# A four-layer graph network on one core: one row per node, product tables and chains down the partitions in place of transposed scans over an edge list

## The reference, cut to what matters

```python
x = ln(x + segment_sum((x @ W0)[src] * rsqrt(deg_out[src]) * rsqrt(deg_in[dst]), dst) + b0)   # layer 0
def conv(x, Wm, We, Wr, b):
    agg = segment_max(x[src] @ Wm + edge_attr @ We, dst)          # 0 for nodes without edges
    return leaky_relu(agg + x @ Wr + b)
x = ln(x + conv(conv(x, W1m, W1e, W1r, b1), W2m, W2e, W2r, b2))   # layer 1, halves a and b
m = relu(x[src]) + 1e-7
a = segment_softmax(m, dst)                                       # per feature
x = ln(x + (x + segment_sum(a * m, dst)) @ Wg + bg)               # layer 2
h = x @ Wa                                                        # layer 3: attention with self loops
x = ln(x + tanh(sum over edges and self of softmax(leaky_relu(a_src[src] + a_dst[dst])) * h[src] + ba))
```

## Time and profile before

| | |
|---|---|
| runs | 5404.59, 5427.97, 5431.95 us (median 5427.97) |
| profiled execution, span from first to last instruction | 5313.3 us |
| median of the runs less the span | 114.7 us |
| DVE busy | 3742.5 us (70%) x10898 |
| POOL busy | 3265.5 us (61%) x2855 |
| PE busy | 3222.1 us (61%) x14728 |
| ACT busy | 2565.5 us (48%) x4956 |
| DMA | 658.31 MB moved, mean 124 GB/s |
| longest wait by kind | PE for the gathered rows of layers 2 and 3: 623.6 us in 87 waits |

### The profile page before, as it was taken

How to read it: one execution, slowest core, us unless ns; L and a number is a source line. 1 busy time by engine, 2 the same in 40 slices (tenths; PEclk the granted TensorE clock), 3 DMA queues, 4 the chain that set the end, 5 groups by cost and what they waited for, 6 DMA issues and landing times. The chain is left out here.

```text
span 5313.3 us, 65383 instructions
## 1 busy us (share of the span) xinstructions
PE 3222.1 (61%) x14728; PEld 2578.5 (49%) x14728; DVE 3742.5 (70%) x10898; ACT 2565.5 (48%) x4956; POOL 3265.5 (61%) x2855
## 2 busy tenths in 40 slices
PE   3344226666657777566666456556664866776664
PEld 1122126666645555444455356555553655555553
DVE  4465348888846676566667699999995866766665
ACT  0000015545535555455556566666663655555554
POOL 7677345555445666445554577777764777777776
PEclk7676655555568888777777666666665555555555
DMA  5444776666557777566666233333333322222221
GB/s 111 100 93 97 51 90 174 169 165 172 161 151 226 229 237 230 167 177 183 178 182 179 69 101 110 100 98 101 110 97 74 73 67 63 64 72 62 64 70 39
DMA packets 596466, 658.31 MB, mean 124 GB/s; under 512 B 251637, under 2 KB 520151, under 8 KB 596406
## 3 DMA queue, kind: packets, MB, share of 16 engines
q1 hardware_dynamic: 451112, 527.29, 32.1%
q0 software_dynamic: 87808, 128.37, 12.8%
q10 hardware_dynamic: 57486, 2.01, 2.5%
HBM read 431.63 MB, written 252.08 MB: 129 GB/s over the span
## 5 line engine op out<-in xcount | busy, mean ns | idle before, releaser
L433 POOL DMA_INDIRECT l_G<-t,l_idx x784 | 998.1, 1273 | 301.9 <-issue 222.8
L569 POOL DMA_INDIRECT l_gs<-xa,l_idx x392 | 394.7, 1007 | 439.1 <-DMA l_idx<-ids 257.0
L433 POOL DMA_INDIRECT l1b_G<-tc,l1b_idx x392 | 372.9, 951 | 381.4 <-PE l1b_psT L441 214.4
L433 POOL DMA_INDIRECT l1a_G<-t,l1a_idx x392 | 402.7, 1027 | 320.4 <-DMA l1a_idx<-src_rows 152.0
L1575 POOL DMA_INDIRECT out<-l_s_out,l_sidx x392 | 466.4, 1190 | 191.5 <-issue 115.2
L441 PE MATMUL l_psT<-ident,l_G 128*96 128x128 f32 x784 | 187.3, 419 | 640.2 <-DMA l_G<-t,l_idx 623.6
L433 POOL DMA_INDIRECT G<-x_pad,idx x392 | 422.6, 1078 | 170.4 <-issue 130.5
L441 PEld LDWEIGHTS l_psT<-ident,l_G 128*96 128x96 f32 x784 | 141.3, 194 | 670.0 <-DMA l_G<-t,l_idx 354.0
L394 PE MATMUL counts<-hot_lo,hot_hi 128*98 128x512 bf16 x784 | 238.6, 472 | 353.4 <-DVE hot_hi L333 220.3
L330 DVE TENSOR_SCALAR hot_lo<-iota_lo,lo 128x512 bf16<-128x512 f16 x784 | 238.0, 378 | 265.0 <-remote 231.7
L1775 PE MATMUL l_psA<-l_wt,l_T 97*128 97x97 f32 x784 | 298.8, 481 | 115.3 <-ACT l_e_out L1706 93.1
(11 more groups left out here) (272 smaller groups left out, 10146.4 us busy)
## 6 DMA issues: line engine op xcount, KB each, us to landing
t<-l1b_normal SPq DMA_DIRECT2D x98, 384.0 KB
l_xs<-t SPq DMA_DIRECT2D x98, 384.0 KB
xa<-x_pad SPq DMA_DIRECT2D x49, 384.0 KB
xd<-G SPq DMA_DIRECT2D x49, 384.0 KB
l_xn<-x_pad SPq DMA_DIRECT2D x49, 384.0 KB
l_xd_in<-xd SPq DMA_DIRECT2D x49, 384.0 KB
t<-l_xn_out SPq DMA_DIRECT2D x49, 384.0 KB
t<-l_xe_out SPq DMA_DIRECT2D x49, 384.0 KB
```

What stands on the lines that cost most here:

```text
L433: pool.indirect_dma_start(tile[:, u, q, :], None, table, bass.IndirectOffsetOnAxis(idx[:, u, q:q + 1], 0)).then_inc(done[u], 16)
L569: pool.indirect_dma_start(gs[:, u, q, :], None, xa, bass.IndirectOffsetOnAxis(idx[:, u, q:q + 1], 0))\
```

## The change

The whole kernel is written anew. There is **one row per node** in every table.

- **Layout.** Edge and row e of 50,176 lies in partition e // 392, column e % 392 (`K = 392`); a chunk is 8 columns of all 128 partitions. A node's running value lies at its last edge; nodes without edges are given to the other edges' rows. `FIX`, a 50th chunk of one column, holds per partition the one node whose edges began in an earlier partition.
- **`numbering`** (new) makes the table row -> node (`nidx`): 392 pairs of one-hots (L313 128x392, L315 128x128, f16), PE adds up, then shifts by bits (9 rounds each of about 4 and 2 and 2 passes of some 392 columns).
- **`entry`** (new): POOL gathers x by `nidx` into `O`, 128 x 393 x 96, which stays in SBUF from here on. DVE makes one-hots of `src` (L509, L514) for the degrees and then of `nidx` with two high parts (L506 and L511) to invert the table, PE adds up. Then, for 49 chunks, SP loads x transposed (`x_t`, laid out by the host as is `edge_k`), PE multiplies by W0, ACT scales the rows into `y` and SP stores `y0`, 98 wide, in which each row also has its own number: layer 0's gather brings the new indices along (`k.src`).
- **Product tables.** Each layer multiplies its nodes by the next layer's weights ahead of the store (`t1`, `t2` for messages, `r1`, `r2` for the root part; 128x192 products, L869 and L1176), so gathered rows are summands already. In layer 2 the table holds exp(m) and exp(m)*(m+eps), 192 wide; softmax becomes a quotient of two sums, without a running maximum.
- **Chains in place of scans.** Per chunk 8 SCALAR_TENSOR_TENSORs of 96 to 98 columns (192 in layer 2), each of which takes the one before it as input and has a `drain` behind it. Each chunk of chain results is also stored to `hist`, for the fix-up at the end.
- **PSUM sums in layer 1.** PE multiplies the gathered rows by `ident` (two 384-column matmuls) and adds the edges' products to them; the chain reads its input there. `psE` has one buffer.
- **No loops.** All 49 chunks are written out on all engines; `chunks` and `Fori` are gone.

Counts of indirect DMAs: 393 in each of entry, layers 0, 1a, 1b, 2 and 3 (gathers) and 393 scatters; before 7 x 392. The diff, cut to its core:

```diff
-                dve.wait_ge(rows_in[u], 16 * LOADS * (i + 1))
-                dve.wait_ge(messages, c + 1)
-                dve.tensor_tensor_scan(S[:, u, :], restart[:, u, :], psT[0:D, :], S[:, 1 - u, CH - 1:CH],
-                                       ALU.add, ALU.max).then_inc(scanned, 1)
-                dve.drain()
-                dve.wait_ge(own_ready, c + 1)
-                dve.tensor_tensor(z[:, :], S[:, u, :], psX[0:D, :], ALU.add).then_inc(added, 1)
-                dve.drain()
-                if warm:
-                    dve.wait_ge(returned, c - 1)
-                    if first:
-                        dve.wait_ge(kept[u], 32 * i)
-                dve.scalar_tensor_tensor(conv[:, u, :], z[:, :], LEAK, z[:, :], ALU.mult, ALU.max)\
-                   .then_inc(leaked, 1)
-
...
+            for c in range(NCH):
+                if c >= 2:
+                    dve.wait_ge(tallied, c - 1)
+                for q in range(Q):
+                    dve.tensor_scalar(hot_lo[:, c % 2, q, :], k.iota_lo[:, :],
+                                      lo[:, c * Q + q:c * Q + q + 1], None, ALU.is_equal)
+                    made = dve.tensor_scalar(hot_hi[:, c % 2, q, :], k.iota_hi[:, :],
+                                             hi[:, c * Q + q:c * Q + q + 1], None, ALU.is_equal)
+                made.then_inc(hot_ready, 1)
...
+                                                 ALU.is_equal)
+                        if both:
+                            dve.tensor_scalar(hot_hi[:, u, 0, q, :], k.iota_hi[:, :], hi[:, at],
+                                              rid_hi[:, at], ALU.is_equal, ALU.mult)
+                            made = dve.tensor_scalar(hot_hi[:, u, 1, q, :], k.iota_hi[:, :], hi[:, at],
+                                                     rid_lo[:, at], ALU.is_equal, ALU.mult)
+                        else:
+                            made = dve.tensor_scalar(hot_hi[:, u, 0, q, :], k.iota_hi[:, :], hi[:, at], None,
+                                                     ALU.is_equal)
...
+                    for i in range(4):
+                        q = 4 * h + i
+                        made = act.activation(y[:, u, q, 0:D], psY[h][:, i * 128:i * 128 + D], ACT.Copy,
+                                              scale=inv_out[:, c * Q + q:c * Q + q + 1])
+                    made.then_inc(scaled, 1)
...
+            for c in range(NCH):
+                s = c % SLOTS
+                if c >= SLOTS:
+                    pool.wait_ge(joined, c - SLOTS + 1)
+                    pool.wait_ge(kept[s], 16 * (c // SLOTS))
+                for q in range(Q):
+                    at = c * Q + q
+                    pool.indirect_dma_start(G[:, s, q, :], None, y0,
+                                            bass.IndirectOffsetOnAxis(k.src[:, at:at + 1], 0))\
+                        .then_inc(gathered[s], 16)
...
+                S = tile(c)
+                dve.wait_ge(edged, 2 * c + 2)
+                dve.drain()
+                for q in range(Q):
+                    at = c * Q + q
+                    if at:
+                        before = S[:, q - 1, :] if q else tile(c - 1)[:, Q - 1, :]
+                        done = dve.scalar_tensor_tensor(S[:, q, :], before, k.restart[:, at:at + 1], E[:, q, 0:D],
+                                                        ALU.add, ALU.max)
+                    else:
+                        done = dve.tensor_copy(S[:, 0, :], E[:, 0, 0:D])
+                    if q < Q - 1:
+                        dve.drain()
+                done.then_inc(chained, 1)
...
+                if c < NCH:
+                    for q in range(n):
+                        at = c * Q + q
+                        last = dve.scalar_tensor_tensor(R[:, s, q, :], tile(c)[:, q, :], k.lastok[:, at:at + 1],
+                                                        R[:, s, q, :], ALU.mult, ALU.add)
+                else:
+                    last = dve.tensor_tensor(r, F[:, :, :], r, ALU.add)
+                dve.drain()
+                if first:
+                    dve.scalar_tensor_tensor(r, r, LEAK, r, ALU.mult, ALU.max).then_inc(joined, 1)
+                else:
+                    dve.scalar_tensor_tensor(r, r, LEAK, r, ALU.mult, ALU.max)
...
+            pe.wait_ge(ready, 1)
+
+            def edges(c):
+                s = c % SLOTS
+                pe.wait_ge(gathered[s], 128 * (c // SLOTS + 1))
+                if c >= 1:
+                    pe.wait_ge(chained, c)
+                for h in range(2):
+                    pe.wait_ge(edge_in[h], 16 * (c + 1))
+                    half = slice(h * Q // 2, (h + 1) * Q // 2)
+                    pe.matmul(E[:, half, 0:D], k.ident[:, :], G[:, s, half, :], start=True, stop=False,
+                              skip_group_check=True)
+                    for i in range(Q // 2):
+                        last = pe.matmul(E[:, h * Q // 2 + i, 0:D], edge[:, h, i * 128:(i + 1) * 128], we[:, :],
+                                         start=False, stop=True, skip_group_check=True)
...
+
+            def turn_rows(c):
+                pe.wait_ge(joined, c + 1)
+                if c >= 1:
+                    pe.wait_ge(copied, c)
+                turn(pe, psT, lambda q: R[:, c % HELD, q, :], tiles(c), k.ident).then_inc(turned, 1)
+
+            def multiply(c):
+                pe.wait_ge(copied, c + 1)
+                if c >= 1:
+                    pe.wait_ge(taken_r, c)
+                for q in range(tiles(c)):
+                    last = pe.matmul(P[:, q, 0:2 * D], xT[:, q * 128:(q + 1) * 128], w[:, :], start=True, stop=True)
+                last.then_inc(multiplied, 1)
...
+            def root(c):
+                u, n = c % 2, tiles(c)
+                act.wait_ge(measured, c + 1)
+                act.activation(lg[:, u, 0:n], mv[:, u, 0:n, 1], ACT.Ln, bias=k.eps[:, :])
+                act.drain()
+                act.activation(rstd[:, u, 0:n], lg[:, u, 0:n], ACT.Exp, scale=-0.5).then_inc(rooted, 1)
...
+            def invert(c):
+                u, n = c % 2, tiles(c)
+                v = inv[:, u, 0:n, :]
+                act.wait_ge(chained, c + 1)
+                if c >= 2:
+                    act.wait_ge(turned_v, c - 1)
+                act.activation(v, tile(c)[:, :, 0:D], ACT.Ln)
+                act.drain()
+                act.activation(v, v, ACT.Exp, scale=-1.0).then_inc(inverted, 1)
...
```

2708 lines of the change are left out of this document (1378 added, 1330 removed).

## The result

| | before | after |
|---|---|---|
| median of 4 runs | 5429.49 us (5404.59 to 5431.95) | 5648.85 us (5643.57 to 5653.49) |
| ratio, 95% interval | | **1.042 (1.040 to 1.045)** |
| profiled execution, span | 5313.3 us | 5645.6 us |
| DVE, POOL, PE, ACT busy | 3742.5, 3265.5, 3222.1, 2565.5 us | 2792.7, 2679.7, 2140.1, 2060.2 us |

The change is slower by 4.2%. 4850 us was forecast, with a range of 4400 to 5330, so the prediction was wrong, in its sign too. The work did shrink: VectorE does 950 us less, TensorE 1082 us less, DMA moves 522 MB in place of 658. The time went into gaps.

A forecast was written before the change was run, and what follows sets the result against it. No engine was full; GpSimd's gathers set a floor of 10.0 us a chunk (20.2 in layer 3), with scans and stalls above. Stages 280+740+565+635+655+745+1035 plus 85 for stalls gave 4740, plus 115: 4850 us; range 4400 to 5330.

The forecast's parts named there:

- the 1000 to 1070 us that would show it right: Layer 3: sign of a right forecast, the layer taking 1000 to 1070 us with GpSimd the busiest engine.
- lie beside the one-hots: Entry: the 393 gathers, 490 us of GpSimd, run alongside VectorE's one-hots within the stage's 740 us.
- so I charge nothing: Entry: no time added for VectorE's one-hots holding up gathers, since the new one-hots are all TENSOR_SCALAR.
- Instruction supply: All stages: unnamed stalls from written-out code, 12 us for each of 7 stages, 85 in all, nothing mid-stage.
- Rival E: Five layer stages: straight code stalls on instruction fetch mid-stage, 10.9 us once in 4 chunks, 667 us: 5515 us; chance 0.08.
- D: Entry: back-to-back one-hots starve the gathers, so the stage takes 980 instead of 740 us: 5090 us; chance 0.06.
- A: Layers 0, 1a, 1b, 2: GpSimd's floor paces every layer at 10.2 us a chunk, 402 less: 4450 us; chance 0.13.
- B: Layers 1b and 2: Ln and Exp share one ScalarE table, saving loads, 235 us less: 4615 us; chance 0.02.
- C: Layers 1a and 0: TensorE's clock stays slow, 14.0 and 11.1 us a chunk, adding 120: 4970 us; chance 0.08.
- The 115 us: Whole kernel: the old median's excess over its profiled span, kept and added to the forecast span of 4740 us.

The follow-up runs named there:

- window: Changed kernel; in the entry GpSimd waits, before a chunk's gathers, until those of the chunk before the previous one have landed: 4559.32 us, session without stalls.
- late_gathers: Changed kernel with the entry's gathers begun only after the first one-hot pass: 5639.24 us, one run, with stalls.
- paced_entry: Changed kernel; in the entry only, GpSimd waits for a chunk's 8 gathers to land before issuing the next 8: 5211.43 us, ratio 0.961, with stalls.
- one_pause_b: Changed kernel, GpSimd waiting for each chunk's 8 gathers to land, in layer 3 for the 8 scatters before the next gathers: 4849.53 us, ratio 0.894, with stalls.
- l3_one_pause: Same kernel as one_pause_b, changed kernel with pauses in every stage, one per chunk in layer 3, session without stalls: 4744.30 us, ratio 0.990.

## Why the prediction was wrong, point by point

| stage | forecast | without stalls | with stalls |
|---|---|---|---|
| numbering | 280 | 222 | 222 |
| entry | 740 | 685 | 1122 |
| layer 0 | 565 | 541 | 786 |
| layer 1a | 635 | 648 | 733 |
| layer 1b | 655 | 639 | 654 |
| layer 2 | 745 | 764 | 770 |
| layer 3 | 1035 | 1038 | 1336 |
| stalls | 85 | none found | in the stages |

**The prices of the stages held.** Where nothing stalls, the sum of the stages (4740 less the 85, 4655) came out at 4537, each layer within 5%. Gathers took 0.95 to 0.96 us, the links of layer 1a 0.31 us, layer 3 fell within the 1000 to 1070 us that would show it right, and layer 2 was bound by ScalarE (644 of 764 us busy). The numbering was priced 58 us too high. The gain that was forecast, 578 us, didn't come out there either: without stalls before takes 4794 us and `window` 4559, 235 us less. The baseline of 5428 us had stalls of its own in it, and the prediction set a sum without stalls against it.

**The step that failed** is a price of nothing for what gathers do to the other engines, in two terms. In the entry the 393 gathers "lie beside the one-hots", and only whether VectorE holds them up was asked ("so I charge nothing"): 740 us were forecast, 1122 measured, 685 without stalls. And "Instruction supply" charged stalls without a releaser 12 us in each of 7 stages "and nothing to the middles": 85 us, where the stalls cost 1086 in all, 437 of them in that entry. Rival E had their look (gaps in mid-stage) and a time near the result, 5515, but the wrong cause: `late_gathers` moves them with the gathers, and `paced_entry` removes them, with the code unrolled as before. So it got 0.08 for the wrong reason, and the argument against it, sound as it was against instruction fetch, was taken as an argument against the stalls. The rule cited from the Trainium skill, Runtime: NRT & Kernel Launch, "Instruction fetch mechanics" (fetching ahead in straight code is mostly hidden), isn't contradicted: the same code ran without such gaps at 4559 us.

**The other rivals.** D didn't occur: beside the one-hots of `window` a gather took 984 ns. A didn't: the layers stayed above GpSimd's 10.2 us a chunk even without stalls (11.0 to 15.6). B didn't either: ScalarE was busy 13.1 us a chunk of layer 2 (643.95/49), the four table loads in it. C didn't decide: the granted clock was 0.62 with stalls and 0.67 without in layer 0, 0.69 and 0.70 in 1a.

**The trace had shown it.** In the earlier trace rows L330, the old one-hots, stood idle 265.0 us, of which 231.7 "remote", beside gathers. I used its busy time for a price and passed over its wait. In order of time it reads, in the trace of before:

```profile
311.17 0.94 POOL L433 DMA_INDIRECT G<-x_pad,idx  x1 [0.30 <-issue]
...
314.83 4.29 DVE L330 TENSOR_SCALAR hot_lo<-iota_lo,lo 128x512 bf16<-128x512 f16 x16 [22.28 <-remote]
```

A gap of 22 us on VectorE at the end of a run of at least 10 gathers, and 14 more of 11.6 to 23.7 us in the 601 us of `degrees`. Rival D asked whether one-hots hold up gathers; the other direction, gathers holding up one-hots, wasn't asked. By these rows the entry's first pass, with its 393 gathers in one run, was the place to fear most, and it was the worst.

**The 115 us** between before's span and its median were carried over to the forecast. The changed kernel's median lies 3 us above its span. The execution with the span of 5313.3 us isn't among the runs beside it (5404.59 us and more), but fits those of the session in which before took 5285 to 5346 us. So the term was most likely a difference between two sessions.

## What to carry to other kernels

An idle time that the profile gives to "remote" or "issue" deserves a question: what runs beside it, and does the change make that run longer? It isn't a price by itself, though: in `one_pause_b` most landings are missing from the trace (25,330 updates against 60,037 in `l3_one_pause`), and waits that `l3_one_pause` puts down to a DMA aren't named there. Compare the length of the stage. When indirect DMAs of GpSimd follow one another without a gap beside a busy VectorE or TensorE, try a wait for the landing of each 8: here it gave the changed kernel 14% for one line a stage, the kernel before nothing, and without stalls it cost 4%. And where the kernel before itself takes two different times in two sessions, compare within a session only.

## What of the hardware was not expected

- In sessions with stalls, gathers 1.25 to 1.40 us apart, after 6 (layer 0) or 15 (entry) in a row, make VectorE and TensorE end their instructions late, VectorE's 1.40 us apart, for up to 27 us past the last gather (746 to 773 us). On ScalarE I found no such spacing. What fills up isn't shown. The recorded semaphore updates are a hint. Of landings there are 1.4 per us in the stalled first pass and 12.4 in the first pass of `window`, for 16 per gather and 0.8 gathers per us in both; in the whole trace 20,073 against 60,034. And from 500 to 700 us all recorded updates together come to 1.43 per us, two per 1.40 us. Every timed run here was traced, so the recording itself may be what stalls; whether the stalls exist in a run that isn't traced is open.
- Back-to-back 16-bit SCALAR_TENSOR_TENSORs held one gather for 311 us; 16-bit TENSOR_SCALARs between 128 and 392 columns did not (984 ns in `window`, 1247 in `one_pause_b`), a 512 wide TENSOR_TENSOR in each group stretched it to 1.22 us.
